# A Mamba layer with a routed expert FFN: x_proj, the shared FFN's last rows and the expert merge in column groups, four scatter buffers, a 21st weight slot and transposes in the routing tail

## The reference, cut to what matters

```python
x = x + xattn(ctx, layernorm(x))        # selective scan; the normalised x is the gate z
x = x + ffn(layernorm(x))               # 64 experts, top 6, and a shared expert

# xattn, for each batch
x = silu(causal_conv4(ctx @ in_proj.T) + conv_b)             # 512 channels
dt_low, Bm, Cm = split(x_proj @ x, [16, 32])                 # 48 rows
dt = softplus(dt_proj @ dt_low + dt_b)
state = state * exp(dt * A) + (dt * u) * B                   # 512 x 16 states, over 512 positions
y = (sum_n state * C + D * x) * silu(z)

# ffn, 2048 tokens
scores = softmax(x @ gate_w.T); w, i = top_k(scores, 6)      # each expert takes up to 64 tokens
y[token] += w * (silu(t @ w_gate[e]) * (t @ w_up[e])) @ w_down[e]      # 512 -> 352 -> 512
y += (silu(x @ sw_gate) * (x @ sw_up)) @ sw_down             # 512 -> 704 -> 512
```

## Time and profile before

| | us |
|---|---|
| median of 3 runs | 1051.31 |
| lowest, highest | 1051.05, 1052.87 |
| the profiled execution | 1055.68 |
| its span in the trace | 1053.9 |
| busy PE, DVE, ACT, POOL | 896.8, 604.6, 503.7, 562.3 |

### The profile page before, as it was taken

The page is one execution under the profiler, slowest core; times in us unless marked ns, Lnnn a source line. Parts: engine busy times, 40 slices in busy tenths (PEclk is TensorE's granted clock), DMA queues, the critical chain, the costliest instruction groups (busy, mean ns, idle before and its releaser), DMA issues.

```text
span 1053.9 us, 12293 instructions
## 1 busy us (share of the span) xinstructions
PE 896.8 (85%) x4063; PEld 481.7 (46%) x4063; DVE 604.6 (57%) x863; ACT 503.7 (48%) x867; POOL 562.3 (53%) x318
## 2 busy tenths in 40 slices
PE   6466747667899797999789959999999999998995
PEld 3144535454554464545544555444444444444431
DVE  4598999889788888988897843122122212111111
ACT  4688646797676777766764232212221221121211
POOL 0487998968988978869865701122222322122211
PEclk9567655688999988999899968999999999999998
DMA  8552444425233543333545585899999999999995
GB/s 299 180 174 86 141 141 145 151 85 189 99 120 140 195 147 106 120 120 109 179 141 190 178 310 203 317 388 400 398 386 397 399 396 388 397 393 395 388 387 131
DMA packets 68362, 250.51 MB, mean 238 GB/s; under 512 B 10522, under 2 KB 13094, under 8 KB 68044
## 3 DMA queue, kind: packets, MB, share of 16 engines
q1 hardware_dynamic: 54660, 225.96, 56.2%
q0 software_dynamic: 7744, 18.88, 7.3%
q10 hardware_dynamic: 5896, 4.90, 1.4%
HBM read 230.54 MB, written 19.17 MB: 237 GB/s over the span
## 4 chain that ended last, share of the span: by engine, by line
PE 56%; DVE 14%; DMA 12%; ACT 8%; issue 8%; POOL 2%; POOLq 0%; SPq 0%; DVEq 0%; ACTq 0%
PE ps L812 13%; PE ps L664 13%; PE ps L849 11%; DMA out_rows<-xn,idxs 7%; PE ps L873 6%; DVE ps L1234 5%; PE ps L825 4%; DVE arena L1241 3%; PE ps L881 2%; PE ps L893 2%; DVE arena L1260 2%; ACT ps L1043 2%; DMA out_rows<-arena 2%; DMA out_rows<-so_or_scores 2%; DMA arena<-bc_rows 1%
## 5 line engine op out<-in xcount | busy, mean ns | idle before, releaser
L1466 POOL TENSOR_TENSOR arena<-arena 128x1024 f32<-128x1024 f32 x128 | 299.7, 2357 | 73.0 <-DVE arena L555 38.5
L664 PE MATMUL ps<-ident,arena 128*128 128x128 f32 (+2 forms) x1408 | 244.0, 327 | 95.2 <-POOL arena L1471 25.1
L664 PEld LDWEIGHTS ps<-ident,arena 128*128 128x128 f32 (+2 forms) x1408 | 204.3, 180 | 201.5 <-issue 84.6
L1043 ACT ACTIVATE ps<-arena,An 128x511 f32<-128x511 f32 x256 | 165.2, 680 | 100.7 <-DVE ps L1242 82.2
L1234 DVE TENSOR_TENSOR_SCAN ps<-ps,arena 128x1024 f32<-128x1024 f32 x84 | 192.1, 2287 | 17.0 <-ACT ps L1043 16.0
L812 PE MATMUL ps<-xnT,sw 128*128 128x512 f32 (+1 forms) x328 | 157.6, 624 | 12.2 <-ACT arena L1004 10.5
L849 PE MATMUL ps<-arena 128*64 128x352 f32 x968 | 160.0, 462 | 0.8 <-ACT arena L933 0.8
L1480 POOL DMA_INDIRECT arena<-xn_rows,idu x32 | 34.2, 1069 | 218.1 <-DVE wcol L1379 133.5
L1471 POOL TENSOR_TENSOR arena<-arena 128x1024 f32<-128x1024 f32 x44 | 103.5, 2352 | 60.8 <-DVE arena L1234 60.5
L849 PEld LDWEIGHTS ps<-arena 128*64 128x64 f32 x968 | 70.9, 137 | 81.4 <-issue 79.3
L1241 DVE TENSOR_TENSOR arena<-ps,arena 128x1024 f32<-128x1024 f32 x84 | 102.5, 1220 | 2.2
(11 more groups left out here) (160 smaller groups left out, 974.1 us busy)
## 6 DMA issues: line engine op xcount, KB each, us to landing
arena<-bc_rows SPq DMA_DIRECT2D x128, 512.0 KB, 4.6
arena<-in_L_ffn_w_down SPq DMA_DIRECT2D x60, 768.0 KB, 22.5
arena<-in_L_ffn_w_gate SPq DMA_DIRECT2D x61, 704.0 KB, 22.7
arena<-in_L_ffn_w_up SPq DMA_DIRECT2D x60, 704.0 KB, 21.3
arena<-in_x SPq DMA_DIRECT2D x4, 1024.0 KB, 6.6
xn_rows<-xn ACTq DMA_DIRECT2D x4, 1024.0 KB, 5.5
out_rows<-arena SPq DMA_DIRECT2D x4, 1024.0 KB, 5.2
extra<-in_L_ffn_w_up SPq DMA_DIRECT2D x4, 704.0 KB, 18.8
```

What stands on the lines that cost most here:

```text
L664: return nc.tensor.matmul(dst, src, ident[0:k, 0:k], is_transpose=True, **kw)
L1043: a = nc.scalar.activation(ps[:, 2 * (c % 2) + n, 1:L], dt[k][:, 1:L], ACT.Exp, scale=An[:, k, NB * g + n:NB * g + n + 1])
L1466: G.tensor_tensor(R[c % RING], dtu[k][:, None, :].to_broadcast([P, NB, L]), Brep[n % REPS], ALU.mult)\
```

## The change

- In batch 0, ScalarE copies the first half of the transposed in_proj weights and VectorE the second; the bias vector is transposed before in_proj, the other parameters stay behind its second chunk, in other banks. Chunk 1's softplus of batch 0 and the z statistics are placed after scan 0.
- x_proj takes each chunk of u as it is ready, in two column groups (rows 0 to 47 and 64 to 111 of PSUM) of 256 positions each, with six transposes of the identity ahead of each chunk in batch 0; two copies evacuate it.
- The shared expert's last 64 rows are computed in two column groups, each with half of the tokens; `hs` holds them as 128 partitions of 256 columns, and sw_down's last rows are loaded twice.
- 44 transposes of the identity (`warm`) in batch 3 after the last `yT`.
- The merge writes only the 64 rows of the pair's first expert, as two column groups of 256 columns, copied back into `yw`, which is scattered itself; `yw` and `idxs` have four buffers. The ids are transposed for 64 columns. The shared tiles are added in two DMAs of two tiles instead of four.
- 21 weight slots instead of 20; the last two wait for the end of `xn` and of the output stores.
- Times in all four tables are new. Of batch 3, `sp out` is now placed ahead of pieces 7 to 9; VectorE's last two `sdown` of batch 2 move, the last behind scan 127. `EXTRA` has 18 steps instead of 20.

```diff
+WIDTH = [L] * (IS // P) + [L // 2]
+HALF = IS % P
+FILL = 6
+TAILFILL = 44
-ASLOTS = 19
+ASLOTS = 20
 FIRST = {
-    "act xdt": [-14.9, -13.3, 0.99, 2.55],
+    "act xdt": [-16.83, -1.15, 0.99, 2.55],
-    "pool c": [-13.61, -10.93, 2.64, 4.09],
+    "pool c": [-13.61, 0.1, 2.64, 4.09],
-    "pool sp": [-13.31, -10.76, 3.28, 4.67],
-    "pool dt": [-12.79, -10.73, 3.3, 4.91],
-    "pool dtu": [-11.7, -9.33, 5.24, 5.65],
+    "pool sp": [-13.36, 0.15, 3.28, 4.9],
+    "pool dt": [-12.79, 0.2, 3.3, 4.91],
+    "pool dtu": [-11.7, 0.25, 4.94, 5.65],
+    "dve zstats": [0.4, 1.3, 2.21, 2.49],
 LATE = {
-    "dve sdown": [57.55, 58.8, 60.04, 61.27],
-    "sp out": [62.71],
+    "dve sdown": [59.24, 61.24, 61.24, 63.3],
+    "sp out": [64.66],
 LAST = {
+    "pe warm": [37.0],
-    "sp out": [33.09],
+    "sp out": [29.97],
...
-EXTRA = [0, 4, 6, 12, 18, 20, 24, 26, 36, 44, 52, 76, 84, 88, 90, 100, 108, 116, 118, 120]
+EXTRA = [0, 4, 6, 12, 18, 20, 24, 26, 36, 52, 56, 84, 88, 90, 100, 104, 116, 124]
...
-            load(swd[0:IS % P, NI - 1, :], sw_down[(NI - 1) * P:IS], s["sw_in"])
+            for n in range(2):
+                load(swd[n * HALF:(n + 1) * HALF, NI - 1, :], sw_down[(NI - 1) * P:IS], s["sw_in"])
...
+            def shared_mm(bank, w, k, c):
+                args = dict(start=(k == 0), stop=(k == HC - 1))
+                if c < NI - 1:
+                    return nc.tensor.matmul(ps[:, bank, :], w[:, k, c * P:(c + 1) * P], xnT[:, k, :], **args)
+                for n in range(2):
+                    mm = nc.tensor.matmul(ps[n * HALF:(n + 1) * HALF, bank, 0:L // 2], w[:, k, c * P:c * P + HALF],
+                                          xnT[:, k, n * L // 2:(n + 1) * L // 2], **args)
+                return mm
+            def shared_down(bank, k, c):
+                rows, cols = slice(0, P), c * P
+                if k == NI - 1:
+                    n, c2 = divmod(c, LT // 2)
+                    rows, cols = slice(n * HALF, (n + 1) * HALF), c2 * P
+                return nc.tensor.matmul(ps[:, bank, :], hs[rows, k, cols:cols + P], swd[rows, k, :],
+                                        start=(k == 0), stop=(k == NI - 1))
...
                 elif kind == "xdbl":
-                    pe.wait_ge(s["u_ready"], DC * (b + 1))
                     for k in range(DC):
-                        mm = nc.tensor.matmul(ps[0:DR + 2 * NS, bank, :], xpT[:, k, :], u[k],
-                                              start=(k == 0), stop=(k == DC - 1))
+                        if b == 0:
+                            for n in range(FILL):
+                                transpose(ps[:, 3, 0:P], ident[:], start=True, stop=True)
+                        pe.wait_ge(s["u_ready"], DC * b + k + 1)
+                        nc.tensor.matmul(ps[0:DR + 2 * NS, bank, 0:L // 2], xpT[:, k, :], u[k][:, 0:L // 2],
+                                         start=(k == 0), stop=(k == DC - 1))
+                        mm = nc.tensor.matmul(ps[P // 2:P // 2 + DR + 2 * NS, bank, 0:L // 2], xpT[:, k, :],
+                                              u[k][:, L // 2:L], start=(k == 0), stop=(k == DC - 1))
...
+                elif kind == "warm":
+                    claim(bank)
+                    for n in range(TAILFILL):
+                        transpose(ps[:, bank, 0:P], ident[:], start=True, stop=True)
...
             def merge(q):
-                nc.tensor.matmul(ps[:, 6 + j, :], same[j], yw[j], start=True, stop=True).then_inc(s["merged_mm"], 1)
+                for n in range(2):
+                    mm = nc.tensor.matmul(ps[n * CAP:(n + 1) * CAP, 6 + j, 0:H // 2], same[j],
+                                          yw[q % 4][:, n * H // 2:(n + 1) * H // 2], start=True, stop=True)
+                mm.then_inc(s["merged_mm"], 1)
...
+                    if b == 0 and c == 1:
+                        act.wait_ge(s["pre_t"], 1)
+                        copy(winT[:, 0, :], ps[:, 0, :], s["winL_ready"])
...
             def evac_merged(q):
                 act.wait_ge(s["merged_mm"], q + 1)
-                if q >= 2:
-                    act.wait_ge(s["scat"], 16 * scattered(q - 2))
-                copy(ys[q % 2], ps[:, 6 + q % 2, :], s["ys_ready"])
+                nc.scalar.copy(yw[q % 4][0:CAP, 0:H // 2], ps[0:CAP, 6 + q % 2, 0:H // 2])
+                copy(yw[q % 4][0:CAP, H // 2:H], ps[CAP:P, 6 + q % 2, 0:H // 2], s["ys_ready"])
...
             def weighted(q):
-                if q >= 2:
-                    dve.wait_ge(s["merged_mm"], q - 1)
-                V.tensor_scalar(yw[q % 2], ps[:, 6 + q % 2, :], wcol[q % 3][:], None, ALU.mult).then_inc(s["yw_ready"], 1)
+                if q >= 4:
+                    dve.wait_ge(s["scat"], 16 * scattered(q - 4))
+                V.tensor_scalar(yw[q % 4], ps[:, 6 + q % 2, :], wcol[q % 3][:], None, ALU.mult).then_inc(s["yw_ready"], 1)
```

391 lines of the change are left out of this document (198 added, 193 removed).

## The result

The changed kernel takes 1042.26 us (median of 11 executions, 1040.21 to 1050.32); the kernel before took 1055.53 in the executions beside them (11, 1051.05 to 1059.06). The ratio is 0.9893, 95% interval 0.9867 to 0.9919: faster by about 1.1%, where 2.1% were forecast (22 us, 1029 from 1051). The time lies inside the range by less than 1 us. The forecast's 1029 stands on a median of three runs; against the median of the eleven its 22 us would be 1033.5, and the measured difference is 13.3 us. The profiled execution took 1043.6 us, its span is 1041.9, 12.0 less than before.

A forecast was written before the change was run, and what follows sets the result against it. No one engine bounds over half the time; TensorE's queue mostly paces the scan phase, the rings the expert phase. -1 - 10 - 5 - 6 = -22 from 1055.68 gives 1033.7, median 4.4 lower: 1029; range 1014 to 1043.

The forecast's parts named there:

- Prologue: Up to scan 1: B/C store held by shared weights, first loads near 37.3, scan 1 at 48.5 before 49.76; -1 us.
- its own bound of +2: Prologue's slow limit: the z statistics fully on the path, +2 us.
- Rival (a): Prologue gains in full, the ring does not hold the store: 8 us more, 1021 us; chance 0.10.
- Scan phase: Shared expert's column groups shorten chain matmuls by 9.6 us, x_proj 1 in all; taken -10, between -17 and +3.
- a bound of -3: Scan phase: batch 2's sdown adds behind the last scan take two VectorE waits on TensorE out of the last steps.
- (b): Scan phase gives nothing: VectorE, GpSimd or the new order takes TensorE's place; 1039 us; chance 0.18.
- (d): The column groups don't run side by side: 1040 us; chance 0.04.
- the prediction's bound: Scan phase, tiling-mode drain: at most four new switches a batch at 0.48 us each, giving -5 instead of -10.
- Routing tail: 44 transposes raise TensorE's clock before the logits, first expert matmul at 655.8; store move up to +1; taken -5 us.
- Rival (c): Routing tail: transposes don't raise the clock, xnT starts 3 us later, +3 instead of -5: 1037 us; chance 0.06.
- Expert phase: Rings bound it; 21st slot -2.2, shorter scatter queue at the end -3.6; taken -6, between -9 and +2.
- rival (e): Expert phase slower: waits for weights drop TensorE to half clock in each turn from about turn 20, 1059 us; chance 0.07.

The follow-up runs named there:

- e1: Changed kernel with the shared expert's weights loaded behind the third Brep/Crep pair instead of before the B/C store: 1036.22 us, ratio 0.9824.
- e10: Changed kernel with batch 2's twelve sdown matmul groups and four adds back at their times of before: 1047.34 us, ratio 0.9946.
- e9: Changed kernel with x_proj of batches 1 to 3 whole as before, batch 0 still by chunks: 1043.66 us, ratio 0.9879.
- e8: Kernel before with the change's new times and EXTRA, without x_proj by chunks, column groups or identity transposes, with 20 weight slots: 1058.83 us, ratio 1.0027.
- e4: Changed kernel with batch 3's output stores placed behind pieces 7 to 9 again: 1044.31 us, ratio 0.9889.
- the combination: Changed kernel with shared weights loaded later, 66 tail transposes and batch 3's stores back behind pieces 7 to 9: 1029.07 us, ratio 0.9748; again 1032.57, 0.9805.
- e7: Kernel before with only the shared expert's last 64 rows in two column groups and sw_down's last rows loaded twice: 1046.61 us, ratio 0.9926.
- e2: Changed kernel with 66 instead of 44 transposes of the identity in the routing tail: 1044.23 us, ratio 0.9893.
- e5: Changed kernel with five more identity transposes ahead of gate and up in each of the expert phase's 32 turns: 1048.24 us, ratio 0.9947.
- e14: The combination with shared items spread over 24 turns instead of 28 and 18 identity transposes in the last turn: 1028.05 us, ratio 0.9776.

## Why the prediction was right or wrong

**Prologue (forecast -1, measured +2.4 at scan 1, +4.2 at scan 4).** Right in its mechanism, wrong in size, and past its own bound of +2. The store was held by the ring and the gain of x_proj lost. From scan 0 to scan 1 were 8.8 us, as forecast. The first loads landed near 40.8, not 37.3: I had timed them by the bytes and forgotten that SP waits for the store's landing before it issues them, which before took 1.6 us and now 8.2. Rival (a) was false, and e1 shows why: without the weights ahead scan 1 comes 6.5 us sooner. That fits the Trainium skill (DMA: Bandwidth & Descriptors, Queues, rings and completion order), by which each DMA engine takes a ring's descriptors in order; the 1.6 and 8.2 us agree.

**Scan phase (forecast -10, measured -15.6).** The matmuls were sized rightly: L677 and L679 together 42.5 us in batch 1's stretch (38.4 and 4.1), forecast 42.5. The shared rows alone gave 6.6 of the 9.6 that the chain's shares promised. What carried it further was the moved `sdown`, called a bound of -3 and worth 7.2 behind scan 112 (e10: 65.4 us there, all kernels with the move and the shared rows 58.2). x_proj, priced at 1 in all, was 4 in one batch and 1 to 3.5 at the end (e9). The new order as a whole, taken at nothing, gave 6.7 behind scan 112 and lost 5.7 ahead of it (e8). Ahead of scan 112 the parts don't add up, and the profiled executions of nearly the same scan phase lie up to 10 us apart. Rivals (b) and (d) were false. By the row, 32 records of the column groups take 4.1 us where 16 full ones took 7.7 (two twelfths of the earlier trace rows). The two of a pair start 0.01 us apart. Around 307 us the first of them starts 0.52 us after a full record, where full ones follow each other by 0.43, and the next transpose 0.31 us after the last pair, where pairs follow by 0.21: some 0.1 us a switch. The Trainium skill (TensorEngine Tiling (Array Packing), Key Properties) states a drain at a change of the tiling mode; if this is it, it costs a fifth of the 0.48 us that the prediction's bound took.

**Routing tail (forecast -5, measured +2.0).** The step that failed. The prediction let the burst start at 617.3 at half clock, as before from 93.05, and raise it. In the changed kernel the clock was already full when the burst began, at 606.6, and fell behind it, since it ended 2.8 us too early. The prediction saw this move in the scan phase and not what its matmuls do ahead of the last `yT`: `xnT` 1.7 us later in every kernel with the move, and with the clock 5.0 us (e10). So `xnT` started 14.8 us after the last scan where 13.4 was taken, and from there to the end of the logits were 10.0 us where 5.9 was taken. The second miss is the store, where I took up to +1: 2.4 (e4). With the store back and the clock held the combination's tail is 45.9, 4.2 under before; but e7, without transposes and with the old order, had 45.5, so what they win depends on whether the clock would have risen anyway. Rival (c) came near the tail's number (+3) for a wrong reason. 66 transposes, 7.37 us with nothing else on TensorE, left the clock at 1.00 until 620 (e2): a second row against the rule of the Trainium skill (TensorE: Matmul & The Clock Gate, Part 4: PE-mode transpose) that a transpose does not count as TensorE being busy.

**Expert phase (forecast -6, measured -2.5).** The rings are the bound (e5). To the last byte it is 1.6 us less where the slot was to give 2.2; one piece less moves in that time (144.9 for 145.7 MB), but kernels with 21 slots take 374.2 to 378.1, so the slot's share isn't shown. The end gave 0.9 of 3.6: the queue does not catch up, since the second add of 512 KB takes 13 us at 991.59 and stands only five scatters before the end, and rival (e)'s clock, false for the whole phase (TensorE waited ten times for weights, and the clock fell in three short stretches), was true for the one down that counts, 4.43 instead of 2.80 us. With both mended the end comes 12.4 us after the last byte, forecast 12.8 (e14).

**The sum.** The stages missed by +5.2, -5.6, +7.0 and +3.5 us. Single profiled executions were added, so the scan phase's and the end's share in this rest on executions that vary; the tail's miss repeats in every kernel with 44 transposes and the moved `sdown` (49.7 to 52.1). That the time still lies in the range is partly luck: the scan phase gained by a term that the sum had at nothing. The last 4.4 us of the forecast, the median under the profiled execution, came from three runs; over eleven the median is 0.2 under it.
